# Output projection ahead of a batch's second phase, and the transposed outputs copied by DVE, in the attentions of layers 1 to 3

## The reference

```python
Q, K, V = norm(x) @ Wq (+bq), ctx @ Wk (+bk), ctx @ Wv (+bv)     # 16 heads of 8
scores = einsum('bhqd,bhkd->bhqk', Q, K) / sqrt(8)               # layer 1: masked
attn = softmax(scores)
out = einsum('bhqk,bhkd->bhqd', attn, V)                         # then heads side by side
x = x + out @ Wo (+bo)
```

## Time and profile before

| | us |
|---|---|
| median of 3 runs | 681.62 |
| lowest and highest run | 676.5 and 682.86 |
| time of the profiled execution | 684.64 |
| its span, first to last instruction | 682.7 |
| PE busy over the span | 589.8 |
| DVE busy | 442.2 |
| ACT busy | 300.3 |
| POOL busy | 198.9 |

### The profile page before, as it was taken

How to read it: one execution, slowest core, us unless ns; L and a number is a source line. 1 busy time by engine, 2 the same in 40 slices (tenths; PEclk the granted TensorE clock), 3 DMA queues, 4 the chain that set the end, 5 groups by cost and what they waited for, 6 DMA issues and landing times.

```text
span 682.7 us, 17655 instructions
## 1 busy us (share of the span) xinstructions
PE 589.8 (86%) x7057; PEld 379.4 (56%) x7057; DVE 442.2 (65%) x1207; ACT 300.3 (44%) x520; POOL 198.9 (29%) x314
## 2 busy tenths in 40 slices
PE   6687788669999998888998998899799899899893
PEld 3355556137856664245676555577467466466452
DVE  4746656868464536897665666465776776876872
ACT  2323224001135341642655483455467467476372
POOL 6511105022051002005203754420431430430563
PEclk9989979769999999999999999999999999999998
DMA  6780000800060000000000115300232132131220
GB/s 149 204 267 2 1 2 18 261 16 13 16 234 2 2 2 1 0 1 0 2 3 24 33 43 178 115 2 26 64 89 71 48 89 65 48 96 49 56 58 16
DMA packets 45296, 40.39 MB, mean 59 GB/s; under 512 B 13107, under 2 KB 36695, under 8 KB 45088
## 3 DMA queue, kind: packets, MB, share of 16 engines
q1 hardware_dynamic: 40304, 29.87, 14.1%
q0 software_dynamic: 3584, 8.76, 5.2%
q10 hardware_dynamic: 1328, 0.66, 0.4%
HBM read 30.71 MB, written 8.81 MB: 58 GB/s over the span
## 4 chain that ended last, share of the span: by engine, by line
PE 68%; DVE 18%; issue 5%; ACT 3%; DMA 3%; POOL 1%; DVEq 0%; POOLq 0%; ACTq 0%
PE psum L2032 8%; PE psum L2006 7%; PE psum L657 7%; PE psum L667 6%; PE psum L2016 5%; PE psum L719 4%; PE psum L634 4%; PE psum L731 2%; PE psum L582 2%; PE psum L936 2%; DVE Mp L495 2%; PE psum L1450 2%; DVE scr L1129 2%; PE psum L687 1%; DMA scr<-y_d,rowi 1%
## 5 line engine op out<-in xcount | busy, mean ns | idle before, releaser
L392 ACT ACTIVATE scr<-psum 128x1024 f32<-128x1024 f32 x64 | 65.5, 1023 | 100.7 <-PE psum L687 37.5
L1567 ACT ACTIVATE b1r<-big 128x512 f32 x160 | 87.9, 621 | 35.1 <-DVE be L1773 28.6
L495 DVE TENSOR_REDUCE Mp<-psum 128x8 f32<-128x1024 f32 x64 | 77.9, 1221 | 32.5 <-PE psum L694 15.8
L657 PE MATMUL psum<-scr 32*128 32x256 f32 x512 | 76.5, 420 | 7.7 <-issue 2.7
L367 POOL TENSOR_TENSOR scr<-KT,hmask 128x256 f32<-128x256 f32 x64 | 39.6, 645 | 142.1 <-DVE scr L1369 42.3
L667 PE MATMUL psum<-Qa,scr 32*128 32x128 f32 x1024 | 78.5, 294 | 0.3 <-ACT scr L392 0.3
L667 PEld LDWEIGHTS psum<-Qa,scr 32*128 32x128 f32 x1024 | 65.8, 196 | 2.3 <-issue 1.1
L582 PE MATMUL psum<-fill,identb 128*128 128x512 bf16 x242 | 64.5, 407 | 0.0
L657 PEld LDWEIGHTS psum<-scr 32*128 32x128 f32 x512 | 47.0, 193 | 28.1 <-issue 19.4
L1926 DVE COPY scr<-psum 128x512 f32<-128x512 f32 x48 | 33.2, 692 | 38.0 <-PE psum L2016 37.8
L2016 PEld LDWEIGHTS psum<-ident,scr 128*128 128x128 f32 x232 | 24.6, 142 | 47.3 <-issue 25.8
(11 more groups left out here) (406 smaller groups left out, 1225.0 us busy)
## 6 DMA issues: line engine op xcount, KB each, us to landing
y_d<-scr SPq DMA_DIRECT2D x36, 130.0 KB
big<-in_L_ffn_W SPq DMA_DIRECT2D x2, 2048.0 KB, 9.8
big<-in_L_ffn_W SPq DMA_DIRECT2D x8, 512.0 KB, 9.9
big<-in_L_ffn_W SPq DMA_DIRECT2D x1, 4096.0 KB, 13.9
b1r<-in_L_ffn_b SPq DMA_DIRECT2D x1, 2048.0 KB, 10.5
scr<-y_d,rowi POOLq DMA_INDIRECT x36, 3.3
scr<-in_ctx SPq DMA_DIRECT2D x1, 512.0 KB, 5.2
x<-in_x ACTq DMA_DIRECT2D x1, 512.0 KB, 5.9
```

Source lines behind the costliest of these rows:

```text
L392: act.activation(PT[i % 2][:, c, :], pair(WU), ACT.Exp, scale=SCALE).then_inc(S(f"exp{c}"), 1)
L495: dve.tensor_reduce(Mpe[:, :, :, :, c, DH], pair(2 * c).rearrange("p (r b j k) -> p r b j k", r=2, b=2, j=2), AX.X, ALU.max, negate=True). ...
L657: ins = pe.matmul(bank[2 * e + r][:, 2 * P * c:2 * P * c + 2 * P], QT[rows, c, i, :], Km[rows, i % KB, c, :, :].rearrange("p v k -> p (v k)"),
L1567: ins = act.activation(W2d[d % len(W2d)][:, F * u:F * u + F], W2[k.layer][:, bass.ds(e * F, F)], ACT.Copy)
```

## The change

For layers 1 to 3 and batches i = 2 to 7, PE runs out_transpose(i-2) between attend(i-1, 0) and attend(i-1, 1), and out_project(i-2) after attend(i-1, 1) and ahead of B(i). The copy to oT of batches 0 to 5 goes from ACT's queue to DVE's, at the head of DVE's work of batch i. The last two copies (batches 6 and 7) stay on ACT. DVE's residual(i-2) comes ahead of the statistics of batch i-3.

```diff
@@ act_attention
-                if i >= B or (i > 1 and L > 0):
+                if i >= B:
                     copy_oT(i - 2)
@@ dve_attention
+            def copy_oT(i):
+                dve.wait_ge(S("oT_ps"), n0 + i + 1)
+                dve.tensor_copy(oT[:, :], outs(i)[:, 0:P]).then_inc(S("oT_copied"), 1)
...
+                if 1 < i < B and L > 0:
+                    copy_oT(i - 2)
                 if i + 1 < B:
...
+                if i > 1:
+                    residual(i - 2)
                 if 2 < i < B and L > 0:
                     dve.wait_ge(S("x_res"), n0 + i - 2)
                     last = tile_stats(dve, [i - 3], x)
-                if i > 1:
-                    residual(i - 2)
@@ pe_attention, batch
                 if i > 0:
                     attend(i - 1, 0)
+                if i > 1:
+                    out_transpose(i - 2)
+                if i > 0:
                     attend(i - 1, 1)
                 if i > 1:
-                    out_transpose(i - 2)
+                    out_project(i - 2)
                 phase(2 * i + 4)
                 if i == 0:
                     pe.wait_ge(S("q_copied"), 4 * L + 4)
-                if i > 1:
-                    out_project(i - 2)
                 if i + 1 < B:
                     turn_maxima(i + 1)
```

## The result

The changed kernel takes 688.33 us in the median of four runs (687.48 to 689.33), the kernel before 682.18 in four (676.5 to 682.86): 6.15 us more by the medians, which is 0.9%. The ratio over the runs is 1.0117, with an interval of 1.0079 to 1.0154 (about 5.4 to 10.5 us). The forecast was 684.5 and 2.9 us more. The clock fall of the earlier trace rows is not in this execution either: the granted clock is 1.00 from 437.00 to 441.00, and from the first scores of layer 3 to its exp(2, 0) it took 16.83 us, where the one of before took 18.46.

The account below looks back on a forecast made before the run. PE was taken to bound the attentions. Each layer pays +1.92 us and gets some back: +1.34 in layers 2 and 3 each, +0.26 in layer 1, in all +2.9, so 684.5 us; range 679.0 to 689.0.

Parts of the forecast that it names:

- The wait for the residual is gone: Ahead of turn_outputs, batches 2 to 6: PE's wait of 0.26 us, 15 times, 3.8 us in all, would leave.
- The exponential takes its place: Between B and A, layers 2 and 3: ACT's exponential holds A at B + 2.54, so only 0.08 us per batch returns.
- who holds A in layer 1: Between B and A in layer 1: PE idles 0.23 us for the shifted queries; B to A 3.03, 0.37 gained per batch.
- The copy is hidden: Between out_transpose and out_project: 0.79 us of copy and hops covered by 0.785 of PE's work, so cost 0.
- DVE has room: DVE's queue behind the copy: maxima end with 0.19 us of room before turn_maxima in layers 2 and 3; cost 0.
- the clock stays: TensorE's granted clock in the attentions: under 1.00 between 331 and 358 would have proved the forecast wrong.
- out_project enters the stretch: +0.32 us by its pitch: PE between A and B: out_project adds 0.32 us in each of batches 2 to 7, +1.92 per layer.
- out_transpose moves inside the attends: same work, same stretch: PE between A and B: placing out_transpose between the two attends adds no time.
- PE's few waits are all there is to gain without removing matmuls: PE in the attentions: busy 25.17 of 27.00 us in layer 2, so only its waits can be gained.
- clock falls: Rival, layers 2 and 3: longer PE idling lowers TensorE's clock, 1.5 us each, three giving 689 or more; chance 0.08.
- DVE as the bound: Rival: PE waits for the copy ahead of out_project and maxima end too late for turn_maxima; 687.5 us, chance 0.08.
- The 0.11 given to more than 1% slower: Whole kernel: chance 0.11 of over 1% slower, from the clock, the worse half of the DVE case and scatter.

Follow-up runs that it names:

- e4: Changed kernel with exp(i, 1) over half of its columns in layers 1 to 3: B to A 2.13 us in layer 2, 2.92 in layer 1; no total given.
- e5: Changed kernel with one additional unread matmul of 512 columns ahead of turn_outputs, between B and A, in layers 1 to 3: 689.66 us, batch stays 5.47.
- e8: Kernel before with out_project behind turn_maxima, writing bank 2, for batches 0 to 4 of layers 1 to 3, residual behind the shifted queries: ratio to before 0.9994.
- e1: Kernel before with only DVE's part: copies of batches 0 to 5 on DVE, residual ahead of the statistics, PE's order as before: ratio to before 1.0040.
- e7: Changed kernel's PE order and residual place, but the copies back on ACT, behind exp(i, 0): ratio to before 1.0087.
- e2: Kernel before with only out_transpose put between the two attends, copy on ACT and out_project behind B as before: ratio to before 1.0028.
- e3: Changed kernel with the attends together again and out_transpose ahead of both, out_project still ahead of B: ratio to before 1.0040.
- e6: Changed kernel with one additional unread matmul of 512 columns ahead of attend(i-1, 0), between A and B, in layers 1 to 3: 698.49 us, batch 5.79.
- e9: Changed kernel with the waits for exp1 and the shifted queries placed behind a phase's first two score matmuls in layers 1 to 3: ratio to before 1.0037.

## Why the prediction was right or wrong

**The wait for the residual is gone**, as forecast: 3.8 us of idle time ahead of turn_outputs left the trace.

**The exponential takes its place**, as forecast: B to A is 2.55 in layers 2 and 3 (2.54 forecast) and 3.03 in layer 1 (3.03). e4 shows the hold by its removal, e5 by filling the idle time at no cost, e8 by freeing the residual's wait in another way and gaining the same 0.08. What I had wrong is who holds A in layer 1: by e4 it is exp1, with the shifted queries 0.11 behind it. And the last two batches gave back more than forecast (batch 6: 2.61 to 2.37, batch 7: 2.67 to 2.29), some 0.9 us for layer 2 in all, where the forecast had 0.58: A(7), which has no scores, follows exp1 by 0.14 and attend(7, 1) by 0.06, where the forecast took 0.26.

**The copy is hidden, DVE has room, the clock stays**, as forecast: the two halves of the attends take the same 0.57, one ahead of out_transpose and one ahead of out_project, which follows the end of the copy by 0.17; the maxima end 0.55 ahead of turn_maxima; the clock is 1.00. e1 and e7 show that the copy's engine makes no difference. The copy's 0.29 us on DVE is near the 0.28 of the row which the forecast took. On ACT it takes 0.27 (e7). So the 0.074 us by which it would be longer on DVE by the Trainium skill (Perfetto Trace Analysis, section Optimizing Scalar/DVE Operations) is not seen: it is 0.02.

**The step that failed is a term of the sum: "out_project enters the stretch: +0.32 us by its pitch", and with it "out_transpose moves inside the attends: same work, same stretch".** A to B grew by 0.53, not 0.32. e2 and e3 split that: out_project takes 0.42 where it now stands, and the split of the attends costs 0.13, of which out_transpose gives 0.02 back. (Before, B started 0.10 behind the end of exp0, as in batch 1, where PE waited for it; so these 0.02 may have been a wait.) In layer 1 it is 0.55. Eighteen times this is 12 x 0.53 + 6 x 0.55 = 9.7 us where the forecast had 5.8. With 3.5 given back in place of 2.8 that makes 6.15 in place of 2.9. So the mechanism was right and its cost mis-sized. With it falls the sentence that PE's few waits are all there is to gain without removing matmuls: the same matmuls take more or less time by what they stand beside.

That 688.33 still lies within the range given, 679.0 to 689.0, is luck: its upper end was meant for clock falls. No rival had the price of the step in its new place. The one with the nearest time (687.5, DVE as the bound) did not happen: PE does not wait for the copy, and with the copy on ACT the kernel takes as long (e7). The 0.11 given to more than 1% slower rested on that rival and on the clock alone, so it, and the 0.86 for no change that can be told, followed from a sum that lacked 3.9 us of cost.

I read a matmul's price in one place, behind the 32-row matmuls of B and ahead of the full-size ones of turn_maxima (out_project 0.32 in layer 2), and took it along. In e8, between two steps of its own form, it takes no more than 0.22 in layer 2 (341.11 to the start of turn_outputs at 341.33). Ahead of B, whose matmuls use 32 rows of the array each, and behind the attends, whose matmuls have 9 columns, it takes 0.42. The trace of before had both prices. In layer 1 out_project stands between full-size mask matmuls and turn_maxima, and takes 0.22 (227.75 to 227.97); in batch 7 of layer 2 it stands between 32-row weights and attend(7, 0), and takes 0.42 (361.94 to 362.36):

```profile
227.75 0.38 PE L740 MATMUL psum<-wo,oT 128*128 128x128 f32 x2
227.97 0.38 PE L707 MATMUL psum<-ident,Mp 128*128 128x128 f32 x2
...
361.94 0.49 PE L740 MATMUL psum<-wo,oT 128*128 128x128 f32 x2
```

The same holds of the attends. In batch 7 attend(7, 0) stands alone ahead of turn_outputs:

```profile
362.36 0.64 PE L719 MATMUL psum<-scr,Va 128*9 128x128 f32 x16
...
362.93 0.66 PE L731 MATMUL psum<-ident,hb 128*128 128x128 f32 x4
```

That is 0.57 for one attend, while 1.01 for two says 0.505 each: cutting the run of 32 costs about 0.13 us. In these runs a further change of form (rows or columns of the array that the matmuls use) costs 0.1 to 0.2 us. e6 bears that out: the additional matmul costs 0.32 where it adds a change and 0.22 in layer 1, where it adds none. The Trainium skill has a rule that bears on this (TensorEngine Tiling (Array Packing), section Key Properties): changing the tiling mode drains the TensorE. The trace agrees in that the price stands where forms meet, 0.1 to 0.2 us; whether draining is what takes that time, no run here shows.

## What to carry to other kernels

Before a step is moved on PE, look at what its new neighbours are, and look up in the trace what it takes wherever it already has such neighbours: where matmuls of different shapes (full, few rows, few columns) meet, each meeting had a price here, so a step belongs among its like, and a step put into a run of others splits that run. A wait that disappears is worth only the distance to the next wait behind it; in the same order of work without that wait (here batch 1) the trace often shows it already. And a step costs nothing only in the stretch where its engine idles for another: move work into such a stretch, not out of it, and place a wait directly ahead of the first instruction that needs it.

## What the runs showed of the hardware that I had not expected

- One matmul of 512 columns costs 0.21 us between two steps of full-size transposes (e5, 343.78 to the next start at 343.99), 0.32 between A and attend in layer 2, and 0.22 in layer 1, where A ends with full-size matmuls (e6).
- PE follows ACT by very different distances: out_project 0.05 us behind the copy (e7), A 0.26 behind exp1 where its scores come first, at A(2) to A(6) in layers 2 and 3 of the changed kernel, although nothing else that A waits for was late there. In e9, where the scores do not wait, the weights follow exp1 by 0.14. Yet B follows exp0 by 0.10 in batch 1 with its scores first, too. Why A takes so long stays open.
